# A decoder layer's last normalisation: twelve consecutive tokens on each of 128 partitions, the last quarter applied by VectorE

## The reference

```python
def _layernorm(x, axis=-1, eps=1e-05):
    m = jnp.mean(x, axis=axis, keepdims=True)
    v = jnp.var(x, axis=axis, keepdims=True)
    return (x - m) / jnp.sqrt(v + eps)

x = _layernorm(x + _L0_attn_ref(x, ...))
x = _layernorm(x + _L0_xattn_ref(x, ctx_1024, ctx_1024, ...))
x = _layernorm(x + _L0_ffn_ref(x, ...))      # this normalisation is what changes
return x                                     # (16, 100, 256), float32
```

## Time and profile before

| | us |
|---|---|
| three runs, median (lowest, highest) | 747.06 (745.37, 747.82) |
| the profiled execution, its own time | 747.7 |
| its span | 745.9 |
| what lies around the span | 1.8 |
| last issue of an add to `accd` by POOL | 720.46 |
| first load of the last normalisation issued | 723.22 |
| first activation of it on ACT | 732.05 |
| end | 745.9 |

### The profile page before, as it was taken

One profiled execution on the slowest core, in us unless ns is written; L12 is line 12 of the kernel. 1 busy time (PEld: TensorE's weight loads), 2 busy tenths in 40 slices (PEclk: granted clock), 3 DMA queues, 4 the chain that ended last, 5 costly groups with the idle time before them and its releaser, 6 DMA issues. The chain is left out here.

```text
span 745.9 us, 15440 instructions
## 1 busy us (share of the span) xinstructions
PE 653.6 (88%) x5196; PEld 517.9 (69%) x5197; DVE 379.6 (51%) x897; ACT 318.7 (43%) x757; POOL 259.8 (35%) x462
## 2 busy tenths in 40 slices
PE   6998976999999999999997266999999999999940
PEld 5888864677777777777775164777777777777730
DVE  2877885777777777777772461222222222222213
ACT  2344342677776777777765002222222222222204
POOL 3334553333344333334321102333343343343123
PEclk9999987999999999999998556999999999999985
DMA  8232115556556555555552530121112111112015
GB/s 233 87 75 79 46 44 148 140 156 174 178 150 189 166 160 162 158 158 158 140 156 67 219 130 29 22 32 34 28 30 36 28 28 37 25 28 35 13 27 149
DMA packets 61146, 73.72 MB, mean 99 GB/s; under 512 B 7769, under 2 KB 52129, under 8 KB 60321
## 3 DMA queue, kind: packets, MB, share of 16 engines
q1 hardware_dynamic: 54944, 65.48, 29.9%
q0 software_dynamic: 6144, 7.48, 6.1%
HBM read 38.25 MB, written 12.39 MB: 68 GB/s over the span
## 5 line engine op out<-in xcount | busy, mean ns | idle before, releaser
L1032 DVE TENSOR_REDUCE cmx<-ps 100x1 f32<-100x361 f32 x256 | 133.8, 532 | 74.0 <-PE ps L576 71.9
L835 ACT ACTIVATE cpr<-ps 121x300 f32<-121x300 f32 x256 | 105.1, 420 | 53.5 <-PE ps L587 52.7
L1544 DVE TENSOR_TENSOR hh<-sg,ps 128x344 f32<-128x344 f32 x64 | 32.8, 513 | 131.4 <-PE ps L1354 131.4
L587 PEld LDWEIGHTS ps<-st 120*121 120x121 bf16 x768 | 81.8, 137 | 20.1 <-issue 5.8
L1292 POOL DMA_INDIRECT accd<-y,si x32 | 51.3, 1604 | 124.9 <-DVE y L1555 124.9
L576 PE MATMUL ps<-st 96*100 96x361 bf16 x256 | 85.7, 338 | 5.7 <-DMA st<-parts 3.3
L1376 PE MATMUL ps<-WD,hT 128*128 x384 | 88.3, 380 | 1.3 <-ACT hT L1420 1.3
L1354 PE MATMUL ps<-WG,xsT 128*128 x256 | 86.0, 459 | 0.6 <-ACT xsT L1409 0.6
L587 PE MATMUL ps<-st 120*121 120x100 bf16 x768 | 82.8, 217 | 2.4 <-ACT st L840 1.6
L1354 PE MATMUL ps<-WU,xsT 128*128 x256 | 84.8, 454 | 0.0
L1376 PEld LDWEIGHTS ps<-WD,hT 128*128 128x128 f32 x384 | 72.8, 190 | 16.0 <-issue 1.8
(11 more groups left out here) (189 smaller groups left out, 1078.8 us busy)
## 6 DMA issues: line engine op xcount, KB each, us to landing
st<-parts SPq DMA_DIRECT2D x192, 115.2 KB, 2.4
WD<-in_wd SPq DMA_DIRECT2D x6, 1024.0 KB, 10.4
cx<-in_ctxT SPq DMA_DIRECT2D x16, 361.0 KB, 5.2
WG<-in_wg SPq DMA_DIRECT2D x8, 688.0 KB, 5.2
WU<-in_wu SPq DMA_DIRECT2D x8, 688.0 KB, 4.7
x_sb<-in_x SPq DMA_DIRECT2D x8, 200.0 KB
x1d<-x SPq DMA_DIRECT2D x8, 200.0 KB
x1Td<-x1T SPq DMA_DIRECT2D x8, 200.0 KB, 3.3
```

Source lines behind the costliest of these rows:

```text
L587: mm = pe.matmul(ps[0:CM, B_T + h % 2, c * L:(c + 1) * L], st[b % NX][:, h, c * CH:c * CH + CM], st[b % NX][:, h, CTX:KQ], start=True, sto ...
L835: act.activation(pr[:, h % (2 * HG), :], ps[0:CM, B_T + h % 2, 0:NCH * L], ACT.Exp).then_inc(exp_ok, 1)
L1032: dve.tensor_reduce(mx[:, half, hh:hh + 1], ps[0:L, B_S + h % 2, 0:CTX], AX_X, ALU.max).then_inc(max_ok, 1)
L1544: dve.tensor_tensor(hh[:, t.par, f * FH:(f + 1) * FH], sg[:, f, :], ps[:, B_U + f, 0:FH], ALU.mult).then_inc(h_ok, 1)
```

## The change

The tokens are laid out another way. `acc` now holds tokens 12p to 12p+11 on partition p, for all 128 partitions (`TP` = 12), in slots 1 to 12. A quarter (`NQ` = 4) is three slots (`QT` = 3), so a partition's share of it is 3 KB in one piece, both in `acc` and in device memory. The 64 tokens left over (`TR`, 1536 to 1599) lie in slot 0 of partitions 0 to 63; they go with the first quarter and are loaded and stored by a DMA of their own. Statistics take 13 instructions of each kind for 16 before. DVE writes minus the mean (`nm`) after each quarter's `bn_aggr`, and POOL forms `shift` from it with one instruction where it took two. ACT applies the first three quarters (4, 3 and 3 instructions), and DVE the last one (3 `tensor_scalar`, subtract the mean and multiply by `rstd`), after which it counts `last_ok`, on which the last store waits. `ohl` and the small tiles get 128 partitions, and POOL sets the unused half of slot 0 in `mv` to zero when the experts stage begins, which makes `const` count to 13.

```diff
+TP = T // P
+TR = T - P * TP
+NQ = 4
+QT = TP // NQ
...
-        ohl = sb("ohl", [L, NBH, P])
+        ohl = sb("ohl", [P, NBH, P])
...
-        acc = ohl[:, :, :].rearrange("p n c -> p (n c)").rearrange("p (b d) -> p b d", d=D)
...
+        acc = ohl[:, :, :].rearrange("p n c -> p (n c)")[:, 0:(TP + 1) * D].rearrange("p (j d) -> p j d", d=D)
...
+        def held(q):
+            return acc[:, 1 + q * QT:1 + (q + 1) * QT, :]
+
+        def tokens(a, q):
+            return a[0:P * TP, :].rearrange("(p j) d -> p j d", j=TP)[:, q * QT:(q + 1) * QT, :]
+
+        def slots(q):
+
+            return range(1 + q * QT if q else 0, 1 + (q + 1) * QT)
...
-                for q in range(4):
-                    sp.dma_start(acc[:, q * QB:(q + 1) * QB, :], a[:, q * QB:(q + 1) * QB, :]).then_inc(acc_ins[q], 16)
...
+                for q in range(NQ):
+                    sp.dma_start(held(q), tokens(a, q)).then_inc(acc_ins[q], 16)
+                    if q == 0:
+                        sp.dma_start(acc[0:TR, 0, :], a[P * TP:T, :]).then_inc(acc_ins[q], 16)
+                for q in range(NQ):
+                    if q < NQ - 1:
+                        sp.wait_ge(res_ok, q + 1)
+                    else:
+                        sp.wait_ge(last_ok, 1)
+                    sp.dma_start(tokens(o, q), held(q)).then_inc(out_sent, 16)
+                    if q == 0:
+                        sp.dma_start(o[P * TP:T, :], acc[0:TR, 0, :]).then_inc(out_sent, 16)
+                sp.wait_ge(out_sent, 16 * (NQ + 1))
...
+                pool.memset(mv[:, 0, :], 0.0).then_inc(const, 1)
...
                     pool.wait_ge(rstd_ok, q + 1)
-                    pool.tensor_tensor(shift[:, s], mv[:, s, 0], rstd[:, s], ALU.mult).then_inc(ve_ok, 1)
-                    pool.wait_ge(ve_ok, 2 * q + 2)
-                    pool.tensor_scalar_mul(shift[:, s], shift[:, s], -1.0).then_inc(shift_ok, 1)
+                    pool.wait_ge(nm_ok, q + 1)
+                    pool.tensor_tensor(shift[:, some], nm[:, some], rstd[:, some], ALU.mult).then_inc(shift_ok, 1)
...
-                for q in range(4):
+                for q in range(NQ - 1):
                     act.wait_ge(shift_ok, q + 1)
-                    for b in range(q * QB, (q + 1) * QB):
-                        r = act.activation(acc[:, b, :], acc[:, b, :], ACT.Identity, bias=shift[:, b:b + 1],
-                                           scale=rstd[:, b:b + 1])
+                    for j in slots(q):
+                        n = P if j else TR
+                        r = act.activation(acc[0:n, j, :], acc[0:n, j, :], ACT.Identity, bias=shift[0:n, j:j + 1],
+                                           scale=rstd[0:n, j:j + 1])
...
                     m.then_inc(mv_ok, 1)
-
-                for q in range(4):
+                    dve.wait_ge(mv_ok, q + 1)
+                    some = slice(1 + q * QT if q else 0, 1 + (q + 1) * QT)
+                    dve.tensor_scalar(nm[:, some], mv[:, some, 0], -1.0, None, ALU.mult).then_inc(nm_ok, 1)
+
+                for q in range(NQ):
                     last_stats(q)
+                dve.wait_ge(rstd_ok, NQ)
+                for j in slots(NQ - 1):
+                    r = dve.tensor_scalar(acc[:, j, :], acc[:, j, :], mv[:, j, 0:1], rstd[:, j:j + 1],
+                                          ALU.subtract, ALU.mult)
+                r.then_inc(last_ok, 1)
```

More of the change, by code:

```diff
@@ L1202, in experts @@
         y = sb("y", [P, 2, D])
-        acc = ohl[:, :, :].rearrange("p n c -> p (n c)").rearrange("p (b d) -> p b d", d=D)
[L1206 to L1211, removed]
+        acc = ohl[:, :, :].rearrange("p n c -> p (n c)")[:, 0:(TP + 1) * D].rearrange("p (j d) -> p j d", d=D)
+        stats = sb("fstats", [P, TP + 1, 6])
+        mv = sb("fmv", [P, TP + 1, 2])
+        nm = sb("fnm", [P, TP + 1])
+        ve = sb("fve", [P, TP + 1])
+        rstd = sb("frstd", [P, TP + 1])
+        mhalf = sb("fmhalf", [P, TP + 1])
+        shift = sb("fshift", [P, TP + 1])
+        def held(q):
[4 more added lines that the diff above has]
+            return range(1 + q * QT if q else 0, 1 + (q + 1) * QT)
         names = ("b_in wd_in set_a const chain dm_ok e2_ok M_ok cnt_mm rh_ok ohl_ok inv_mm lists_ok gi_ok si_ok xT_mm xT_ev "
-                 "gu_mm sg_ok h_ok hT_mm hTa_ev hTb_ev y_mm y_ok added acc_in mv_ok ve_ok rstd_ok shift_ok res_ok st_ok out_sent").split()
+                 "gu_mm sg_ok h_ok hT_mm hTa_ev hTb_ev y_mm y_ok added acc_in mv_ok ve_ok rstd_ok shift_ok res_ok st_ok nm_ok last_ok out_sent").split()
         (b_in, wd_in, set_a, const, chain, dm_ok, e2_ok, M_ok, cnt_mm, rh_ok, ohl_ok, inv_mm, lists_ok, gi_ok, si_ok, xT_mm,
-         xT_ev, gu_mm, sg_ok, h_ok, hT_mm, hTa_ev, hTb_ev, y_mm, y_ok, added, acc_in, mv_ok, ve_ok, rstd_ok, shift_ok, res_ok, st_ok,
+         xT_ev, gu_mm, sg_ok, h_ok, hT_mm, hTa_ev, hTb_ev, y_mm, y_ok, added, acc_in, mv_ok, ve_ok, rstd_ok, shift_ok, res_ok, st_ok, nm_ok, last_ok,
          out_sent) = [sem("e_" + n) for n in names]
@@ L1219, in experts @@
         xs_in = [sem(f"xs_in{u}") for u in range(2)]
-        acc_ins = [sem(f"acc_in{q}") for q in range(4)]
+        acc_ins = [sem(f"acc_in{q}") for q in range(NQ)]
         B_G, B_U, B_H, B_Y, B_X = 0, 2, 4, 6, 7
-        N_CONST = 12
-        QB = NB // 4
+        N_CONST = 13
         def steps(emit, eng):
@@ L1243, in _ @@
                 sp.wait_ge(added, 16 * TILES)
-                a = accd.rearrange("(b l) d -> l b d", l=L)
-                for q in range(4):
-                    sp.dma_start(acc[:, q * QB:(q + 1) * QB, :], a[:, q * QB:(q + 1) * QB, :]).then_inc(acc_ins[q], 16)
-                for q in range(4):
[L1248 to L1251, removed]
+                a, o = accd, out.rearrange("b l d -> (b l) d")
+                for q in range(NQ):
[11 more added lines that the diff above has]
+                sp.wait_ge(out_sent, 16 * (NQ + 1))
             @block.gpsimd
@@ L1308, in _ @@
                 steps(emit, pool)
-                for q in range(4):
+                for q in range(NQ):
                     pool.wait_ge(mv_ok, q + 1)
[L1311 to L1314, removed]
+                    some = slice(1 + q * QT if q else 0, 1 + (q + 1) * QT)
+                    pool.tensor_scalar(ve[:, some], mv[:, some, 1], EPS, None, ALU.add).then_inc(ve_ok, 1)
+                    pool.wait_ge(ve_ok, q + 1)
+                    pool.tensor_tensor(rstd[:, some], ve[:, some], mhalf[:, some], ALU.pow).then_inc(rstd_ok, 1)
                     pool.wait_ge(rstd_ok, q + 1)
-                    pool.tensor_tensor(shift[:, s], mv[:, s, 0], rstd[:, s], ALU.mult).then_inc(ve_ok, 1)
-                    pool.wait_ge(ve_ok, 2 * q + 2)
-                    pool.tensor_scalar_mul(shift[:, s], shift[:, s], -1.0).then_inc(shift_ok, 1)
+                    pool.wait_ge(nm_ok, q + 1)
+                    pool.tensor_tensor(shift[:, some], nm[:, some], rstd[:, some], ALU.mult).then_inc(shift_ok, 1)
             @block.tensor
@@ L1570, in last_stats @@
                 def last_stats(q):
[L1571 to L1574, removed]
+                    dve.wait_ge(acc_ins[q], 32 if q == 0 else 16)
+                    for j in slots(q):
+                        n = P if j else TR
+                        m = dve.bn_stats(stats[0:n, j, :], acc[0:n, j, :])
+                    m.then_inc(st_ok, 1)
                     dve.wait_ge(st_ok, q + 1)
-                    for b in range(q * QB, (q + 1) * QB):
-                        m = dve.bn_aggr(mv[:, b, :], stats[:, b, :])
+                    for j in slots(q):
+                        n = P if j else TR
+                        m = dve.bn_aggr(mv[0:n, j, :], stats[0:n, j, :])
                     m.then_inc(mv_ok, 1)
-                for q in range(4):
+                    dve.wait_ge(mv_ok, q + 1)
+                    some = slice(1 + q * QT if q else 0, 1 + (q + 1) * QT)
+                    dve.tensor_scalar(nm[:, some], mv[:, some, 0], -1.0, None, ALU.mult).then_inc(nm_ok, 1)
+                for q in range(NQ):
                     last_stats(q)
+                dve.wait_ge(rstd_ok, NQ)
[3 more added lines that the diff above has]
+                r.then_inc(last_ok, 1)
 def decoder_layer(nc, x, xT, ctxT, sa_wqT, sa_wqkvT, sa_bqk, sa_bqkv, sa_wop, sa_w2T, sa_b2, wqT, wkT, wvT, woT, bqk, bv,
```

4 lines of the change are left out of this document (2 added, 2 removed).

## The result

| | before | after |
|---|---|---|
| median of 20 runs, us | 745.6 (741.1 to 748.87) | 741.53 (736.89 to 745.04) |
| ratio | | 0.9947, 95% interval 0.993 to 0.9965 |
| span of the profiled execution | 745.9 | 739.2 |
| first load of the last normalisation to the end | 22.7 | 17.3 |

The account below looks back on a forecast made before the run. It took ten of 16 DMA engines working in the last normalisation's transfers as the bound. Terms summed to -5.1 us; from 747.7 that gives 742.6, or 742.0 for the runs' median; 742.3 us was taken, range 740.8 to 745.2.

Parts of the forecast that it names:

- What bounds: Last normalisation's loads and stores: a DMA share of 0.66 and 0.60 means ten of 16 engines work; 128 partitions use 16.
- Packets: Loads and stores of the last normalisation: a 3 KB packet takes 130 ns of engine time, a 1 KB packet 56 ns.
- Loads: Last normalisation: first quarter lands at 727.2, the others at about 728.2, 729.3 and 730.3, always before DVE needs them.
- DVE, POOL, ACT: Last normalisation's compute: DVE 1.62 us and POOL 1.62 us per three-token quarter, ACT 0.52 us per activation, ending at 736.0.
- The end: Stores set the end: third store issued at 736.05, two transfers of 2.08 us together, then 2.7 us, giving 740.8.
- 2.7 start, completion and the program's end: After the last store's issue: of 4.99 us before the change, 2.3 are transfer and 2.7 us stay as a fixed part.
- The memset in the preamble: POOL's extra memset as the experts stage begins: 0.11 us, costed at nothing, with 0.8 us of cover remaining.
- The first: Rival on loads and stores: the 0.6 share is a memory-side limit, rate stays 171 to 190 GB/s, 746.2 us; chance 0.10.
- the second: Rival on loads and stores: a 3 KB packet costs nearly what 8 KB does; at 316 ns, 750.7 us; chance 0.03.
- The third: Rival on the last normalisation: slower completions, ACT and DVE steps give the gain back, leaving -2.3 us, 744.8; chance 0.12.

## Why the prediction was right, point by point

*What bounds.* Right: the transfers, at a share of 0.6. The four combinations of partitions and piece, and the 11 and 16 updates of the semaphores, show that it was the count of engines. The Trainium skill's rule (DMA: Bandwidth & Descriptors, Why a DMA increments its semaphore by 16 and not by 1), 10 engines for 100 partitions and 16 for 128, agrees with 0.60 to 0.66 and 0.85 to 0.92.

*Packets.* 130 ns for 3 KB, measured 128 in the stores. The estimate of 106 ns from the Trainium skill's rate of one engine (DMA: Bandwidth & Descriptors, Specifications) was too low. A 1 KB packet can be cheaper than the 56 ns that I had taken from before: 16 x 0.625 x 7.9 / 1680 = 47 ns in the stores from 128 partitions, and 16 x 0.646 x 7.5 / 1595 = 49 ns in the loads to 100 partitions of the kernel before with the early drain.

*Loads.* First quarter forecast 4.0 us after the issue, measured 3.5. The others were forecast to land 1.04 us apart and never to be waited for; the second came 5.7 us after the first issue, for 5.0 forecast. In six of the ten profiles with 3 KB packets DVE waited for a later quarter (0.2 to 0.7 us). This term was mis-sized, by 0.2 us on the path of the profiled execution and by up to 0.7 in others.

*DVE, POOL, ACT.* Three columns of the power took 0.88 us (forecast 0.9), POOL's steps for a quarter 1.58 from DVE's last aggregate to the shift (1.62), an activation 0.50 on 128 partitions (0.52), VectorE's three scalings 1.06 (1.2 to 1.3), and `nm` was never waited for. ACT started 7.08 us after the first issue, forecast 7.6.

*The end.* This is the step that failed. I kept "2.7 start, completion and the program's end" from before and took the stores to set the end at 17.6 us after the first issue. The stores were done at 15.6: DVE started 0.5 us sooner than forecast, the last store was issued another 0.2 sooner, and from there it took 3.0 us for 4.3. The term of 2.7 us was mis-sized. In the kernel before, the queue was not empty when the last store was issued at 740.91. The packets from 734 us to then:

```profile
DMA packets 978, 0.98 MB, mean 142 GB/s; under 512 B 21, under 2 KB 978, under 8 KB 978
```

Three quarters are 1.23 MB, so 0.25 MB of the third were still to go, at 171 to 200 GB/s about 1.3 us. I counted them as a fixed part, and then added the third quarter's transfer to it once more. What is fixed is shown by the kernel with the layout alone, whose last store was issued at 729.89 + 4.11 - 0.33 = 733.67. There the DMA share just behind that issue is 0.02, so the queue was empty, and the data moved only after it:

```profile
729.89 4.11 SPq L1265 DMA_DIRECT2D out<-ohl  x3
733.60:734.40 0.80, 0.00 (x0) 0.00 (x0) 0.00 (x0) 0.04 (x1) 0.00 (x0) 0.50 0.02 4
L1250 SPq DRAIN  x1: 7/7/7, 736.1 to 736.1; - x1
```

SP was through 2.4 us after the issue, of which 1.04 are transfer, so 1.4 are start, completion and SP's own steps. With it the sum of the prediction comes out: the changed kernel's third store could be issued at 734.0, when ACT was done, and 734.0 + 2.08 + 1.4 = 737.5, which is where the stores were done. Then POOL's drain, which I had not looked at, held the end to 17.3. Two errors of 2.0 and 1.7 us cancelled, so that the length of the tail came out right (17.6 forecast, 17.3 measured) is luck.

*The memset in the preamble* cost nothing: DVE still started on the bias, 1.05 us after POOL's last memset began.

*The rivals.* The first fell with 128 partitions at 275 to 325 GB/s, the second with 128 ns. The third had the right idea at the wrong place: a fixed step did give back part of the gain, 1.5 us by the early drain, but it was neither the completions nor ACT.

## What to carry to other kernels

When a DMA share stands still below 1 with transfers queued, compare it with the share of the 16 engines that the partition count can use (0.6 went with 100 partitions here, 0.85 to 0.92 with 128) before looking at sizes. When a fixed cost is taken from the end of a kernel, see first whether the queue was empty when the last transfer was issued: here half of the 2.7 us was not fixed. When a tail is shortened, look at how every queue ends and not only at the one that ended last: here a drain that had 1.6 us to spare took 1.5 us of the gain. If GpSimd has an idle stretch behind its last indirect DMA, an explicit drain there can take the cost out of the end.

## What the runs showed that I had not expected

- GpSimd's drain is over 5.3 to 5.5 us after the end of its last instruction in a block with indirect DMAs (5.3 to 5.6 us by the profile, which mostly counts it from that instruction's start), and takes 0.5 us at the end of the first block, which has none. With an earlier drain behind the last indirect DMA the later one takes 0.05 to 0.36 us.
- With 128 partitions, 1 KB pieces reach 304 GB/s in the stores, 94% of what 3 KB pieces reach (325).
- The view of waits put POOL's drain down to PE's queue. The drain shows only when one asks for the block's last line.
- What makes the later loads land later in one profile than in another stays open: the third quarter by 1.5 us between the kernel before with and without the early drain, by 0.9 between kernels with 3 KB pieces. The packets of the loads took 56 and 49 ns in the first pair.
